# First layer norm of a transformer layer: scale and shift for two token steps in one GpSimd pass

## The reference

```python
x = x + _layernorm(attn(_layernorm(x)))      # attention without softmax, 16 heads of 8
x = x + _layernorm(ffn(_layernorm(x)))       # top-2 of 8 experts and one shared expert

def _layernorm(x, axis=-1, eps=1e-05):
    m = jnp.mean(x, axis=axis, keepdims=True)
    v = jnp.var(x, axis=axis, keepdims=True)
    return (x - m) / jnp.sqrt(v + eps)
```

## Time and profile before

| what | value |
|---|---|
| time, median of 3 runs | 304.06 us (303.97 to 304.24) |
| span of the profiled execution, first to last instruction | 338.5 us |
| mean granted TensorE clock of the profiled execution | 0.876 of full |
| PE busy | 257.4 us (76%) |
| POOL busy | 186.1 us (55%) |
| DVE busy | 177.7 us (52%) |
| ACT busy | 149.8 us (44%) |

### The profile page before, as it was taken

The page is one execution under the profiler, slowest core; times in us unless marked ns, Lnnn a source line. Parts: engine busy times, 40 slices in busy tenths (PEclk is TensorE's granted clock), DMA queues, the critical chain, the costliest instruction groups (busy, mean ns, idle before and its releaser), DMA issues.

```text
span 338.5 us, 6806 instructions
## 1 busy us (share of the span) xinstructions
PE 257.4 (76%) x1425; PEld 201.2 (59%) x1426; DVE 177.7 (52%) x710; ACT 149.8 (44%) x537; POOL 186.1 (55%) x243
## 2 busy tenths in 40 slices
PE   0985399798978989826039998888997888898670
PEld 0973378687665868625028877676776767774120
DVE  4854697465564747135605555454545545550392
ACT  3874234634445365134305554344544544540270
POOL 5882217775765868727603564655555455564271
PEclk9999658969878597767658999999999999999896
DMA  7780001111101001101231322322222222202963
GB/s 211 228 248 8 0 0 34 33 48 35 41 32 40 32 32 50 56 24 57 65 87 38 84 73 63 87 77 59 77 67 70 79 54 65 67 32 59 325 258 118
DMA packets 28089, 26.34 MB, mean 78 GB/s; under 512 B 6904, under 2 KB 21893, under 8 KB 28066
## 3 DMA queue, kind: packets, MB, share of 16 engines
q1 hardware_dynamic: 21312, 17.35, 17.5%
q0 software_dynamic: 4384, 8.60, 7.6%
q10 hardware_dynamic: 2370, 0.14, 0.4%
HBM read 14.83 MB, written 11.75 MB: 79 GB/s over the span
## 4 chain that ended last, share of the span: by engine, by line
issue 47%; PE 32%; SPq 9%; DMA 3%; DVE 2%; POOL 2%; ACT 2%; another core or an unknown queue 1%; POOLq 0%; DVEq 0%; ACTq 0%
PE bank L1037 9%; PE bank L1021 6%; PE bank L1019 5%; PE bank L1029 5%; PE bank L1020 4%; SPq L374 2%; PE bank L1131 2%; DMA xnT<-expert_results 2%; SPq L365 1%; SPq L380 1%; SPq L357 1%; PE bank L1190 1%; SPq L381 1%; POOL rstd L500 1%; DVE hid L783 1%
## 5 line engine op out<-in xcount | busy, mean ns | idle before, releaser
L549 POOL DMA_INDIRECT expert_results<-eo,rowt x72 | 70.5, 980 | 71.9 <-DVE eo L943 53.9
L518 POOL DMA_INDIRECT expert_rows<-src,slot x64 | 66.7, 1042 | 24.4 <-issue 17.9
L783 DVE TENSOR_TENSOR hid<-sgate,bank 128x256 f32<-128x256 f32 x104 | 43.5, 419 | 62.9 <-ACT sgate L568 40.1
L1037 PE MATMUL bank<-down,hidT 128*128 (+1 forms) x416 | 70.3, 295 | 6.1 <-issue 2.9
L568 ACT ACTIVATE sgate<-bank 128x256 f32<-128x256 f32 x104 | 40.5, 389 | 72.3 <-PE bank L1021 61.0
L1037 PEld LDWEIGHTS bank<-down,hidT 128*128 128x128 f32 x416 | 58.9, 204 | 10.0 <-issue 8.5
L1029 PE MATMUL bank<-ident,hid 128*128 128x128 f32 x208 | 43.9, 295 | 21.7 <-DVE hid L783 18.1
L1029 PEld LDWEIGHTS bank<-ident,hid 128*128 128x128 f32 x208 | 27.2, 149 | 40.8 <-DVE hid L783 24.0
L575 ACT ACTIVATE hidT<-bank 128x256 f32<-128x256 f32 x104 | 40.7, 391 | 12.0 <-PE bank L1029 8.8
L943 DVE TENSOR_SCALAR eo<-bank,rowt 128x128 f32<-128x128 f32 x72 | 24.9, 346 | 26.2 <-PE bank L1037 18.1
L1019 PE MATMUL bank<-gu_hi,rh 128*128 x72 | 35.4, 492 | 3.2 <-DVE rl L927 2.5
(11 more groups left out here) (165 smaller groups left out, 458.7 us busy)
## 6 DMA issues: line engine op xcount, KB each, us to landing
rowt<-expert_rows SPq DMA_DIRECT2D x72, 66.0 KB
X<-n_L_attn_in_sequence_bwc SPq DMA_DIRECT2D x8, 256.0 KB, 5.7
X<-expert_results SPq DMA_DIRECT2D x8, 256.0 KB, 5.9
xnT<-expert_results SPq DMA_DIRECT2D x8, 256.0 KB, 6.5
out<-X SPq DMA_DIRECT2D x8, 256.0 KB, 2.5
expert_results<-eo,rowt POOLq DMA_INDIRECT x72
gu_f<-in_L_ffn_gate_proj_w SPq DMA_DIRECT2D x1, 1024.0 KB, 5.7
gu_f<-in_L_ffn_up_proj_w SPq DMA_DIRECT2D x1, 1024.0 KB, 9.2
```

Source lines behind the costliest of these rows:

```text
L518: nc.gpsimd.indirect_dma_start(rows_d, bass.IndirectOffsetOnAxis(ap=slot[u][:, i, k:k + 1], axis=0), src[u][:, k, i, :], None).then_inc(ro ...
L549: nc.gpsimd.indirect_dma_start(res_d, bass.IndirectOffsetOnAxis(ap=rowt[v][:, P:P + 1].bitcast(U32), axis=0), eo[v % 4][:], None, bounds_c ...
L783: nc.vector.tensor_tensor(hid[v][:], sgate[v][:], gu_ps[v][:, M:2 * M], ALU.mult).then_inc(hid_done, 1)
L1037: last = mm(y_ps[own][v], hidT[v][:, a, :], down[:, e, a, :], start=a == 0, stop=a == MC - 1)
```

## The change

POOL no longer works out scale and shift when one step's statistics are there. It waits for those of two steps and does `vpe`, `nmean`, `rstd` and `shift` for both at once, on 128x8 values. There are 4 rounds of four instructions in the place of 8. The statistics, and the four results, now have a place for every step in tiles of their own, so POOL no longer waits for `xn_done`, and DVE no longer waits for `ln1_c`. `vpe` comes ahead of `nmean` and adds eps with one operation in the place of a multiplication by 1 and an addition. ACT waits for the pair's `shift` and reads its columns. `mhalf` has 8 columns; the later layer norms read its first four. The diff's core:

```diff
-        mhalf = sb("mhalf", [P, G])
-        table_in = sb("table_in", [P, G])
+        mhalf = sb("mhalf", [P, 2 * G])
+        table_in = sb("table_in", [P, 2 * G])
...
-        mv = [sb(f"mv{u}", [P, G, 2]) for u in range(RING)]
+        mv = sb("mv", [P, STEPS * G, 2])
...
+        vpe1 = sb("vpe_ln1", [P, STEPS * G])
+        rstd1 = sb("rstd_ln1", [P, STEPS * G])
+        nmean1 = sb("nmean_ln1", [P, STEPS * G])
+        shift1 = sb("shift_ln1", [P, STEPS * G])
...
-            def norm_shift(mv_u, vpe_u, rstd_u, nmean_u, shift_u, s, base):
-
-                nc.gpsimd.tensor_scalar(nmean_u[:], mv_u[:, :, 0], -1.0, None, ALU.mult).then_inc(s, 1)
-                norm(mv_u[:, :, 1], 1.0, vpe_u, rstd_u, s, base + 1)
-                gp.wait_ge(s, base + 3)
-                nc.gpsimd.tensor_tensor(shift_u[:], nmean_u[:], rstd_u[:], ALU.mult).then_inc(s, 1)
-
-            for s in range(STEPS):
-                r = s % RING
-                after(gp, xn_done, s - RING + 1)
-                gp.wait_ge(mv1_done, s + 1)
-                norm_shift(mv[r], vpe[r], rstd[r], nmean[r], shift[r], ln1_c, s * 4)
+            def norm_shift_of_two(n):
+
+                two = slice(n * 2 * G, (n + 1) * 2 * G)
+                gp.wait_ge(mv1_done, 2 * n + 2)
+                nc.gpsimd.tensor_scalar(vpe1[:, two], mv[:, two, 1], EPS, None, ALU.add).then_inc(ln1_c, 1)
+                nc.gpsimd.tensor_scalar(nmean1[:, two], mv[:, two, 0], -1.0, None, ALU.mult).then_inc(ln1_c, 1)
+                gp.wait_ge(ln1_c, n * 4 + 2)
+                nc.gpsimd.tensor_tensor(rstd1[:, two], vpe1[:, two], mhalf[:], ALU.pow).then_inc(ln1_c, 1)
+                gp.wait_ge(ln1_c, n * 4 + 3)
+                nc.gpsimd.tensor_tensor(shift1[:, two], nmean1[:, two], rstd1[:, two], ALU.mult).then_inc(ln1_c, 1)
+
+            for n in range(STEPS // 2):
+                norm_shift_of_two(n)
             more_constants()
...
-                act.wait_ge(ln1_c, s * 4 + 4)
+                act.wait_ge(ln1_c, s // 2 * 4 + 4)
...
                     dve.wait_ge(x_in[s], 16)
-                    after(dve, ln1_c, (s - RING + 1) * 4)
-                    stats(lambda i: X[:, s % 2, s // 2 * G + i, :], st[r], mv[r], st1_w, mv1_done, s)
+                    stats(lambda i: X[:, s % 2, s // 2 * G + i, :], st[r], mv[:, s * G:(s + 1) * G], st1_w, mv1_done, s)
```

More of the change, by code:

```diff
@@ L117, in build_sandwich @@
         st = [sb(f"st{u}", [P, G, 6]) for u in range(RING)]
-        mv = [sb(f"mv{u}", [P, G, 2]) for u in range(RING)]
+        mv = sb("mv", [P, STEPS * G, 2])
         sumsq = [sb(f"sumsq{u}", [P, G]) for u in range(2)]
[L120 to L123, removed]
+        vpe1 = sb("vpe_ln1", [P, STEPS * G])
+        rstd1 = sb("rstd_ln1", [P, STEPS * G])
+        nmean1 = sb("nmean_ln1", [P, STEPS * G])
+        shift1 = sb("shift_ln1", [P, STEPS * G])
+        vpe = [sb(f"vpe{u}", [P, G]) for u in range(2)]
+        rstd = [sb(f"rstd{u}", [P, G]) for u in range(2)]
         st3 = [sb(f"st3{u}", [P, G, 6]) for u in range(2)]
@@ L499, in norm @@
                 gp.wait_ge(s, base + 1)
-                nc.gpsimd.tensor_tensor(rstd_u[:], vpe_u[:], mhalf[:], ALU.pow).then_inc(s, 1)
-            def norm_shift(mv_u, vpe_u, rstd_u, nmean_u, shift_u, s, base):
-                nc.gpsimd.tensor_scalar(nmean_u[:], mv_u[:, :, 0], -1.0, None, ALU.mult).then_inc(s, 1)
-                norm(mv_u[:, :, 1], 1.0, vpe_u, rstd_u, s, base + 1)
-                gp.wait_ge(s, base + 3)
-                nc.gpsimd.tensor_tensor(shift_u[:], nmean_u[:], rstd_u[:], ALU.mult).then_inc(s, 1)
-            for s in range(STEPS):
-                r = s % RING
-                after(gp, xn_done, s - RING + 1)
-                gp.wait_ge(mv1_done, s + 1)
-                norm_shift(mv[r], vpe[r], rstd[r], nmean[r], shift[r], ln1_c, s * 4)
+                nc.gpsimd.tensor_tensor(rstd_u[:], vpe_u[:], mhalf[:, 0:G], ALU.pow).then_inc(s, 1)
+            def norm_shift_of_two(n):
[9 more added lines that the diff above has]
+                norm_shift_of_two(n)
             more_constants()
@@ L531, in attn_step @@
                     gp.wait_ge(vpe3_done, num(q1, u1) + 1)
-                    nc.gpsimd.tensor_tensor(rstd3[u1][:], vpe3[u1][:], mhalf[:], ALU.pow).then_inc(ln3_c, 1)
+                    nc.gpsimd.tensor_tensor(rstd3[u1][:], vpe3[u1][:], mhalf[:, 0:G], ALU.pow).then_inc(ln3_c, 1)
                 if exists(q3):
@@ L595, in _ @@
                     last = nc.scalar.activation(xn[r][:, i, :], X[:, s % 2, s // 2 * G + i, :],
-                                                ACT.Identity, bias=shift[r][:, i:i + 1], scale=rstd[r][:, i:i + 1])
+                                                ACT.Identity, bias=shift1[:, s * G + i:s * G + i + 1],
+                                                scale=rstd1[:, s * G + i:s * G + i + 1])
                 last.then_inc(xn_done, 1)
```

## The result

The changed kernel took 310.13 us (median of 4 runs, 308.19 to 310.70) against 304.15 us before: a ratio of 1.0169, 95% interval 1.0125 to 1.0213, which is 5.1 us (3.8 to 6.5). This ratio, and those further down, are estimates from the repeated runs and not quotients of the two medians; here the quotient is 1.0197, or 6.0 us. By either the kernel is slower, as forecast, by less than 2%; the forecast was 4.3 us. Its profiled execution has a span of 308.7 us and a time of 310.65.

The account below looks back on a forecast made before the run. POOL's pace (1.87 us a step) and a POOL-ACT-PE-DVE loop bound the first stage, whose delay passes on nearly whole. Loss 2.64 + 2 x (P - 1.04), P = 1.88 for `rstd`: 304.06 + 4.3 = 308.4 us; range 305.9 to 309.6.

Parts of the forecast that it names:

- TensorE's slow start: PE's step 0 at half rate, taken to move along with PE's first matmul, 2.46 us later.
- pair 3: Steps 6 and 7 reach ACT at 23.17 us; their last tile ends at 26.37, against 22.05 before.
- The ring: Loop POOL, ACT, PE, DVE, POOL: later statistics wait behind DVE's copies, so ACT idles 3.3 us ahead of step 4.
- The price of P: POOL's `rstd` on 8 columns taken as 1.88 us; rival 1.04 us, loss 2.6, time 306.7 us, chance 33%.
- all of the 0.84 us is work for each column: In POOL's `rstd`, `pow` time beyond 0.20 us grows with columns: 0.20 + 2 x 0.84 = 1.88 us.
- The first wait, the small operations: POOL's `vpe` waits for step 1's statistics until 7.03 us; `rstd` follows 0.59 later; ACT starts 2.46 us late.
- the case that I gave 8%: Rival: PE's full rate comes later, so step 1 is slow too; loss 4.9 us, time 309 us, chance 8%.
- Nothing behind the stage takes it back: The stage's delay reaches the kernel's end nearly whole; rival, hidden in a later wait: 304.1 us, chance 4%.
- The clock later: Rival: PE's mean clock from 45 to 150 us rises from 0.79 to 0.83, repaying 4.3 us; about 304 us, 6%.
- PE's new idle times in the stage: PE idles ahead of steps 4 and 6; by the skill's clock rule the stage would, if anything, lengthen; no size given.
- The Trainium skill's figure: By some 2.6 cycles an element, four more columns cost POOL's `rstd` next to nothing, leaving it at 1.04 us.

Follow-up runs that it names:

- changed kernel, again: The changed kernel without any edit, run and profiled again beside the kernel before on one chip; ratio 1.0158 (1.0087 to 1.0228).
- the pair wait alone: Against the kernel before: POOL starts two steps only when both have statistics, then does two rounds on 128x4 values; ratio 1.0105 (1.0056 to 1.0153).
- the changed order: Against the changed kernel: DVE does the statistics of all 8 steps ahead of all 8 copies of transposed tokens; ratio to the kernel before 1.0000.
- the kernel before with TensorE warm: Against the kernel before: 26 transposes of the identity on TensorE ahead of its first step, nothing else; ratio 0.9980 (0.9952 to 1.0008).

## Why the prediction was right, and by how much it was off

The median, 310.13 us, lies 0.5 us over the forecast's range of 305.9 to 309.6. By the ratio the time is 304.15 + 5.1 = 309.3, inside it, and the loss is 0.8 us over the 4.3 forecast. The direction and the mechanism were right. Against the first profile the sum was short mainly by one term, TensorE's slow start; in the second that term was as forecast and the stage ended earlier than forecast:

| | forecast | changed kernel, first profile | changed kernel, again |
|---|---|---|---|
| ScalarE's first tile starts | 9.81 | 9.93 | 9.73 |
| `rstd` on 8 columns | 1.88 | 1.67 | 1.67 |
| step 7's statistics end | 20.29 | 21.49 | 20.12 |
| pair 3 reaches ScalarE | 23.17 | 24.20 | 22.83 |
| last tile ends | 26.37 | 27.39 | 26.02 |

- **The ring.** Right, and shown by the pair wait alone, which makes the loss without a wide pow, and by the changed order, which takes ScalarE's later gaps away.
- **The price of P.** 1.67 us, between the ends of 1.04 and 2.08. The reading "all of the 0.84 us is work for each column" was wrong: a start of its own is in it. The sum counts P twice, so it was 0.4 us too high by this.
- **The first wait, the small operations.** From `vpe` to `rstd` 0.65 us, 0.59 forecast; the first tile was within 0.12 us.
- **TensorE's slow start** was the term that was mis-sized. I took it to move along with the first matmul, as it did in the second profile of the changed kernel. In the first it lasted through step 1, and step 7's `mv` came 1.2 us later than forecast. This is the case that I gave 8%, a loss of 4.9 us with 0.6 of it for PE; PE's share was 1.1 (step 0 began 2.6 us late and step 2 ended 3.7 us late), and with the smaller pow it fits the profile better than the forecast does: 4.3 - 0.4 for the pow, + 0.3 for the later statistics of step 1 (7.21 us against 6.93), + 0.1 for the small operations, + 1.1 for PE is 5.4, and the chain came 5.34 us late. How long the slow start lasts is not given by the kernel alone: of the same kernel, one execution has step 1's eight Gram matmuls at 1.92 us and another at 1.32. I should have given the two cases nearly equal chances.
- **Nothing behind the stage takes it back.** Right within what can be told: the stage ended 5.3 us late in the first profile, whose runs give 5.1 by the ratio, and 3.9 us late in the second, whose runs give 5.3 (2.9 to 7.7). Whether 1 us or so comes on top behind the stage is left open, since single executions of one kernel vary by more.
- **The clock later.** The granted clock from 45 to 150 us was 0.87 in the changed kernel's profile and 0.79 in the first of the kernel before, and the changed kernel was slower all the same. The two were taken on unlike chips. On the chips of 337 to 339 us it was 0.84 in the changed kernel's second profile and 0.83 in the kernel before, and in the kernel before with TensorE warm, on the chip of 305.5 us, it was 0.87, as in the changed kernel's first. So no rise of the later clock shows on like chips, and nothing was paid back. Nor did PE's new idle times in the stage cost rate: behind the 1.81 us ahead of step 6, eight Gram matmuls took 1.16 us, as they did behind a wait in the kernel before.
- **The Trainium skill's figure** for a two-input operation (GPSIMD Engine Reference, section 3.1, about 2.6 cycles an element) would, by the estimate in the prediction, have left `rstd` at 1.04 us. It was 1.67. The trace disagrees with using it for `pow`.

## What to carry to other kernels

Before making one engine's work cheaper by doing it in larger batches, follow what its output releases, all the way around, until it comes back as its own input. A batch waits for its last member, and if that stands in another engine's queue behind a wait for an earlier batch's result, the batch size is what closes the loop; the order in that queue is then worth more than the instructions saved. An engine whose lateness cost nothing before can become the bound once its neighbours start later, as TensorE did here with the statistics first.

## What the runs showed of the hardware

- The same kernel took 304 to 305.5 us on some chips and 337 to 339 on others. The first stage was alike. The first load of the routed stage was issued at 171.3 us in the kernel before on a chip of the second kind and at 153.3 on one of the first (that with TensorE warm), so 18 us of the difference had arisen by then; the rest is behind it. The profiles don't say why, and I did not try to find out.
- TensorE's slow start, read from durations, varied between executions: step 1's eight Gram matmuls took 1.40, 1.73 and 1.14 us in three executions in which the first stage is that of the kernel before. So did the load of step 1, whose statistics began between 5.62 and 6.38 us. Together that is an estimated 1 us or more in the date of a stage which such a wait bounds.
- `pow` on GpSimd costs about 0.4 us and 0.16 us a column of 128 values, where a multiplication on 4 or 8 columns is 0.20.
